# Written-out merge orders for the first three and the last three passes of a software-pipelined transformer kernel

## The chip, the cores and the metric

The kernel runs on one core of a Trainium2 chip. The metric is the device time of one execution in microseconds, as the median of three runs.

## The reference, cut to what matters

There are 32 sequences of 256 tokens with 256 features. For each, a cross attention with 16 heads ("conditioning") is computed from `x` and a second input, and two layers of local attention and gated feed-forward follow; `x` is added at the end.

```
c = cond(x, side, lens)                     # 16 heads, keys masked by length, one own key per query
for l in (0, 1):
    q, k, v = split(shift(c) @ wqkv[l])     # 8 heads of 64
    q, k = rotary_xpos(l2norm(q) * qs, l2norm(k) * ks)
    c = c + local_attention(q, k, v) @ wo[l]       # windows of 128, with a mask
    h = layernorm(shift(c)) * g + b
    a, g = split(h @ w1[l] + b1[l])
    c = c + (a * gelu(g)) @ w2[l] + b2[l]
out = x + c
```

## The kernel before

The work of one sequence is cut into 150 steps in four streams. Stream A (57 steps) is the conditioning: `rows`, `project`, `turn_q`, `part`, `own_key`, 16 `score` and 16 `prob` steps with `split`, `turn_max` and `value` between them, and three `mix` steps. Stream R (24, twelve a layer) projects and rotates q and k: `qk`, `rotate`, `combine`, `turn`. Stream S (48) is the local attention: `value_rows`, `scores`, `normalize`, `turn_probs`, `weigh`, `out_proj`. Stream N (21) is the feed-forward: `mean`, `variance`, six `hidden`, two `down`, and a `finish` that adds `x`.

A step has a part on each engine that takes part in it, and many have none on some engine. The four compute engines each run the steps in an order of their own. `ORDER` (line 124) holds it: four cuts and a string of 150 letters. Each letter takes the next step of its stream. The strings describe one pass. In pass i the kernel does the conditioning of sequence i, layer 0 of sequence i-1 and layer 1 of sequence i-2; steps behind a stream's cut are done one pass later still (`body_of`, line 147). There are 32 sequences and `LAGS` is 3, so 35 passes are written out one behind the other (`run`, line 374). In the first three and the last three of them the same string is used and the steps of sequences that don't exist are left out. So pass 0 holds the conditioning of sequence 0 alone, passes 3 to 31 are full, and passes 32 to 34 hold the layers of the last sequences.

Engines wait for each other by semaphores. Every wait names the sequence and the count that it needs, so another order changes no wait. SyncE has its own fixed order of loads (line 492): in pass i it loads the rows of sequence i+1, and then places the split query and key parts of sequence i in `cQT` and `cKT` by twelve transfers (line 458), each behind the part that it moves: three high key parts, two middle ones, three high query parts, one low key part, two middle query parts, the low query part. The first `score` of a sequence waits for all of them. The low parts are made by GpSimd (`part`, line 549), which also does a power for the norms (`rotate`, line 559), sums in `mean` and `variance` (lines 568, 572) and the parts of the maxima (`split`, lines 537 to 544).

Behind the conditioning of sequence 0 each engine calls its `layers_setup` once (TensorE 88 small matmuls at line 719, the vector engine scalings at lines 1055 to 1094).

Lines that the text speaks of: TensorE `project` 744 to 762, `score` 781, `prob` 799, `value` 809, the mix 820 to 834, `finish` 876, `qk` 894, `value_rows` 908, `turn` 928, `scores` 941, `turn_probs` 950, `weigh` 961, `out_proj` 970, `mean` 980, `variance` 983, `hidden` 994, `down` 1007. Vector engine: `part` 1130, the maxima of `score` 1146, `rotate` 1201 to 1218, `hidden` 1283, `down` 1292. ScalarE: `scores` (exponentials) 657, copy of the turned probabilities 661.

Of the kernel before, what the change touches and what calls it, by code (L numbers as in the profile page):

```python
# [97 lines left out]
def head_steps():  # L98
    steps = []
    for u in range(CH + LAG + 2):  # L100
# [22 lines left out]

ORDER = dict(
    PE=((57, 24, 27, 1),
        "SSARASNASSRRAASRSSAASANRNSSAASNAARARAANAANASANAASANAANSSSSASAASASAAARSRRANARSRNAASRSASARNASASASRRANA"
        "SSASASRASSAARNSNNRNANSSNSASSASASAANSSARSRARRSRANSA"),
    DVE=((56, 22, 27, 1),
        "RAARSSASSSSRRASAANSAASRNSSAANAAAAANASAAANNASANASRRASSAASARSRARASASSNNAARAANSSARRAARRRSNSSAAASAAAAAAA"
        "AAAAAASSSSSRSNNSNNNRNSSSSAAASRNSRNSSRRRSSSSSNRAANS"),  # L130
    Activation=((56, 24, 26, 0),
        "NASARSAANSASSSAAAARSRSAAAAANARAARASSNNRNNANSSANRASNSASASSAASSASASAAAARSASARANRRASRNARSAASAAASRSRSAAS"
        "SSSARSARANANNRRNNNSSSSNNSAASSAASSNASASAASRARSRRRAS"),
    Pool=((52, 11, 43, 0),
        "SSASSSSSSSSSSSSASSRRRAAARRRASARRNNNNNNNARNRRRRRSSAAARAAAAARANRAAARAAASAAARSNRRRNSSSSSASSSSSAAAASRSRA"
        "NNSSSNANNAANNASSSAAAANAASSSSSSASNAAAAAANAAAAASAAAS"),
)


# [4 lines left out]
    N=[(1 + l,) + step for l in range(DEPTH) for step in FEED[l]])  # L144


def body_of(engine):

    cuts, letters = ORDER[engine]
    taken = {}  # L150
    for letter, cut in zip(STREAMS, cuts):
        steps = STREAMS[letter]
        taken[letter] = iter([(lag + 1, name, n) for lag, name, n in steps[cut:]] + steps[:cut])
    body = [next(taken[letter]) for letter in letters]
    assert len(body) == sum(len(steps) for steps in STREAMS.values())
    return body


LAGS = 3


# [27 lines left out]
def adaln_ffn_kernel(nc, x, side, lens, wq, bq, wk, bk, wv, bv, cwo, bo, b_prev, b_self,  # L189
                     wqkv, q_scale, k_scale, wo, ln_g, ln_b, w1, b1, w2, b2, consts, out,  # L190
                     seqs):
    with ExitStack() as ctx:
# [181 lines left out]
        def run(eng, engine, step, layers_setup):  # L374

            body = body_of(engine)

            layers = [False]

            def static(i):  # L380
                for lag, name, n in body:
                    if 0 <= i - lag < seqs:
                        if name not in CONDITIONING and not layers[0]:
                            layers_setup()
                            layers[0] = True
                        step(i - lag, name, n)
                        if (name, n) == CONDITION[-1] and not layers[0]:
                            layers_setup()
                            layers[0] = True

            for i in range(seqs + LAGS):
                static(i)

        def copy_probs(eng, copy, seq, l, h):

# [955 lines left out]
```

## Time and profile before

| | |
|---|---|
| median of three runs | 3763.35 us (3762.83 to 3767.95) |
| profiled execution, its own time | 3767.51 us |
| its span, first to last instruction | 3765.3 us |
| TensorE matmuls busy | 3602.7 us (96%) |
| vector engine busy | 2670.4 us (71%) |
| ScalarE busy | 2242.3 us (60%) |
| GpSimd busy | 788.4 us (21%) |
| mean granted TensorE clock | 0.978 of full |

The names in the profile: PE is TensorE, PEld its weight loads, DVE the vector engine, ACT ScalarE, POOL GpSimd, SP SyncE. Start and duration are in microseconds from the start of the span. A matmul in float32 is recorded as two. Busy time of TensorE counts modelled ends, so it is not a measure of how well a matmul does. Passes in the middle repeat every 111.0 us; the full pass 3 starts near 310 and the last full pass, 31, ends near 3529.

### The profile page before, as it was taken

The numbers are of one execution on the slowest core, as the hardware profiler recorded it, in microseconds if no ns is written. First come the engines' busy times: TensorE is split into PE (matmuls) and PEld (weight loads), VectorE is DVE, ScalarE is ACT, GpSimd is POOL, SyncE is SP. The second block draws the span as 40 slices with busy tenths as digits, with TensorE's granted clock in tenths as the row PEclk, the third lists the DMA queues.
The fourth block names the chain that finished last, engine by engine and source line by source line (L and its number), as shares of the span: only waits on it lengthen the run. The fifth ranks groups of instructions, "written<-read, shape, count | busy, mean of one in ns | idle before, by whom it ended". The sixth has DMA issues, their size and how long they took to land.

```text
span 3765.3 us, 58543 instructions
## 1 busy us (share of the span) xinstructions
PE 3602.7 (96%) x20454; PEld 2447.4 (65%) x20454; DVE 2670.4 (71%) x7188; ACT 2242.3 (60%) x5085; POOL 788.4 (21%) x882
## 2 busy tenths in 40 slices
PE   5789999999999999999999999999999999999987
PEld 2456666666666666666666666666666666666655
DVE  2567777777777777777777777777777777777654
ACT  1246566566566666656656656666665665666653
POOL 1122221222222122222122222212222222222110
PEclk7799999999999999999999999999999999999998
DMA  5111110111111011111101111101111110111000
GB/s 144 23 24 23 29 29 20 16 24 29 29 29 29 14 20 26 29 29 29 23 13 24 30 29 29 29 17 19 24 29 29 29 26 13 21 29 24 7 6 9
DMA packets 104608, 99.34 MB, mean 26 GB/s; under 512 B 15276, under 2 KB 103040, under 8 KB 104320
## 3 DMA queue, kind: packets, MB, share of 16 engines
q1 hardware_dynamic: 104320, 95.61, 13.8%
q8 instruction: 168, 2.75, 0.3%
q14 instruction: 120, 0.98, 0.1%
HBM read 35.80 MB, written 8.39 MB: 12 GB/s over the span
## 4 chain that ended last, share of the span: by engine, by line
PE 85%; DVE 7%; issue 3%; ACT 3%; SPq 1%; POOL 0%; DMA 0%; DVEq 0%; ACTq 0%; POOLq 0%
PE ps L994 15%; PE ps L894 12%; PE ps L1007 9%; PE ps L908 6%; PE ps L941 5%; PE ps L961 5%; PE ps L950 4%; PE ps L809 3%; PE ps L970 3%; PE ps L928 3%; PE ps L752 3%; PE ps L762 3%; PE ps L799 3%; PE ps L781 2%; PE ps L834 2%
## 5 line engine op out<-in xcount | busy, mean ns | idle before, releaser
L559 POOL TENSOR_TENSOR inv<-ssq_f,minus_half 128x16 f32<-128x16 f32 x128 | 419.8, 3279 | 1043.9 <-DVE ssq_f L1209 1040.4
L994 PE MATMUL ps<-feed_area,w_s 128*128 128x256 f32 x2560 | 600.7, 382 | 7.3 <-DVE feed_area L1273 6.3
L994 PEld LDWEIGHTS ps<-feed_area,w_s 128*128 128x128 f32 x2560 | 480.5, 191 | 123.2 <-issue 54.1
L657 ACT ACTIVATE attn_area<-attn_area,f_nb,inv 128x128 f32<-128x128 f32 (+1 forms) x1024 | 546.3, 536 | 13.2 <-DVE f_nb L1237 11.6
L1146 DVE TENSOR_REDUCE c_mx<-ps 128x2 f32<-128x512 f32 x512 | 343.2, 687 | 180.5 <-PE ps L781 179.7
L679 ACT ACTIVATE feed_area<-ps,b_s 128x256 f32<-128x256 f32 x320 | 151.0, 473 | 386.3 <-PE ps L994 384.8
L1007 PE MATMUL ps<-feed_area,w_s 128*128 128x256 f32 x1536 | 355.2, 381 | 5.2 <-DVE feed_area L1283 1.5
L610 ACT ACTIVATE cond_area<-ps 128x512 f32<-128x512 f32 x512 | 294.9, 593 | 104.3 <-PE ps L799 103.4
L1233 DVE CUSTOM_DVE_ANT_0 attn_area<-ps,cst 128x128 f32<-128x128 f32 (+1 forms) x1024 | 303.8, 353 | 72.7 <-issue 71.2
L1007 PEld LDWEIGHTS ps<-feed_area,w_s 128*128 128x128 f32 x1536 | 281.7, 190 | 48.9 <-DVE feed_area L1283 14.6
L1283 DVE SCALAR_TENSOR_TENSOR feed_area<-ps,b_s,feed_area 128x256 f32<-128x256 f32 (+1 forms) x384 | 183.8, 479 | 169.0 <-ACT feed_area L679 166.3
L1248 DVE TENSOR_SCALAR attn_area<-attn_area,f_inv 128x128 f32<-128x128 f32 (+1 forms) x1024 | 284.4, 341 | 9.1
L399 DVE COPY attn_area<-ps 128x384 f32<-128x384 f32 x256 | 142.0, 555 | 200.2 <-PE ps L950 200.2
L648 ACT ACTIVATE attn_area<-ps 128x512 f32<-128x512 f32 x256 | 152.0, 594 | 204.7 <-PE ps L928 201.9
L950 PE MATMUL ps<-cst,attn_area 128*128 128x128 f32 x1536 | 251.1, 280 | 11.8 <-DVE attn_area L1248 11.8
L894 PE MATMUL ps<-wqkv_s,X_ffn 128*128 128x512 f32 x512 | 248.5, 608 | 1.4 <-ACT attn_area L637 1.4
L941 PE MATMUL ps<-attn_area 64*128 64x128 f32 (+1 forms) x2048 | 240.0, 352 | 10.2 <-DVE attn_area L399 5.2
L894 PE MATMUL ps<-wqkv_s,X_cond 128*128 128x512 f32 x512 | 245.8, 602 | 0.1
L961 PE MATMUL ps<-attn_area 128*64 128x256 f32 (+1 forms) x2048 | 227.1, 343 | 18.3 <-ACT attn_area L661 17.9
L970 PE MATMUL ps<-attn_area,wo_s 128*128 128x256 f32 x1024 | 240.6, 384 | 2.6 <-ACT attn_area L665 1.7
L637 ACT ACTIVATE attn_area<-ps 128x512 f32<-128x512 f32 x256 | 151.2, 591 | 152.8 <-PE ps L894 152.7
L549 POOL TENSOR_TENSOR cond_area<-cond_area 128x512 bf16<-128x512 f32 x64 | 102.3, 1598 | 588.8 <-DVE cond_area L1127 395.7
(156 smaller groups left out, 6528.4 us busy)
## 6 DMA issues: line engine op xcount, KB each, us to landing
cond_area<-cond_area SPq DMA_DIRECT2D x384, 128.0 KB, 4.2
x_rows<-in_x SPq DMA_DIRECT2D x32, 256.0 KB, 2.8
f_rows<-in_fside_BxSxS SPq DMA_DIRECT2D x32, 256.0 KB, 3.2
res_rows<-in_x SPq DMA_DIRECT2D x32, 256.0 KB, 2.8
out<-res_rows SPq DMA_DIRECT2D x32, 256.0 KB, 2.1
wqkv_s<-in_L_ffn_wqkv SPq DMA_DIRECT2D x2, 1536.0 KB
w_s<-in_L_ffn_w SPq DMA_DIRECT2D x2, 1364.0 KB
cond_area<-cond_area SPq DMA_DIRECT2D x128, 6.0 KB
```

Source lines behind the costliest of these rows:

```text
L559: nc.gpsimd.tensor_tensor(inv[:, l, t, :], ssq_f[:, l, t, :], minus_half[:, :], ALU.pow).then_inc(SL[l]["inv_norm"], 1)
L610: nc.scalar.activation(cpT[:, u % CPB, :], ps[:, c_bank("prob", u), :], ACT.Exp, scale=float(C_SCALE)).then_inc(S["c_probs"], 1)
L657: nc.scalar.activation(soft[:, h % SOFT, lo:hi], soft[:, h % SOFT, lo:hi], ACT.Exp, bias=f_nb[:, l, q, h:h + 1], scale=inv[:, l, q, h:h + ...
L894: last = mm(ps[:, R0, :], shifted(X_in[l])[:, k, t * P:(t + 1) * P], wqkv_s[:, l, k, c * INNER:(c + 1) * INNER], start=(k == 0), stop=(k = ...
L941: last = mm(ps[:, t_bank("scores", 2 * p + j), q * P:q * P + keys], qT[r:r + FDH, p, q * P:(q + 1) * P], kT[r:r + FDH, p, 0:keys], start=T ...
L950: last = nc.tensor.transpose(ps[:, t_bank(name, h), c * P:(c + 1) * P], soft[:, h % SOFT, c * P:(c + 1) * P], ident)
L961: last = mm(ps[r:r + FDH, t_bank(name, p), lo:N], v_s[:, k, h * FDH:(h + 1) * FDH], pT[:, h % 4, c:c + N - lo], start=(k == 0), stop=(k == 1))
L970: last = mm(ps[:, t_bank(name, m), 0:N], wo_s[:, l, h, m * P:(m + 1) * P], oT[:, h, :], start=(h == 0), stop=(h == HP - 1))
L994: last = mm(ps[:, N0 + f % 2, c * N:(c + 1) * N], w1_s[:, l, k, lo:lo + P], hn[:, k, :], start=(k == 0), stop=(k == KD - 1))
L1007: last = mm(ps[:, N0 + m, 0:N], w2_s[:, l, f, m * P:(m + 1) * P], hid[:, f, :], start=(f == 0), stop=(f == HK - 1))
L1146: V.tensor_reduce(c_mx[:, :, u], ps[:, c_bank("score", u), :].rearrange("p (q k) -> p q k", q=TILES), AX_X, ALU.max).then_inc(S["c_max"], 1)
L1233: V.tensor_tensor_reduce(out=soft[:, h % SOFT, lo:hi], in0=ps[:, t_bank(name, h), lo:hi], in1=mask[:, lo:hi], scale=1.0, scalar=3 * NEG, o ...
```

## The change

The four strings of `ORDER` get new letters. TensorE's, the vector engine's and ScalarE's cuts are the same; GpSimd's cuts change, with two of its working steps exchanged. Two new tables, `HEAD` and `TAIL`, hold for each engine one string for the first three passes together and one for the last three together. `edge_of` builds the list of steps of those passes, stream by stream in the old sequence, and takes them in the order of the letters. The place at which `layers_setup` is called is given by a table (`LAST`): behind the last step of the first conditioning in which the engine works.

```diff
 ORDER = dict(
     PE=((57, 24, 27, 1),
-        "SSARASNASSRRAASRSSAASANRNSSAASNAARARAANAANASANAASANAANSSSSASAASASAAARSRRANARSRNAASRSASARNASASASRRANA"
-        "SSASASRASSAARNSNNRNANSSNSASSASASAANSSARSRARRSRANSA"),
+        "SSARASNSSASASARSARSAANARRNNSAANNAANAASAARASSSRANAAASASSSANSAASSAARSARAANARRASRNAASRASSARNARRNASSAASA"
+        "ARSSSAASSRASAANNSNNNSSNSSAASSARSAASSARSRNRARSRANSA"),
...
-    Pool=((52, 11, 43, 0),
...
+    Pool=((57, 10, 22, 0),
...
+HEAD = dict(
+    PE=(
+        "AAAAAAAAAAAAAAAAAAAAAAAAAAAAAAAAAAAAAAAAAAAAAAAAAAAAAAAAAARARRAAARRSARARASAARRRRAARAAAAASAASAAAAAAAA"
...
+TAIL = dict(
+    PE=(
+        "SSRSSSSRSRSSRSRSNSSSSSSSRSSRNSNRSRRSNRNRNSNSNSNNRSSNSRSSSRRRNSNRSNNNNSNSRSSNSSSSSNSSRSRRNRSRSNSSSSSS"
+        "NSSSSSNSNNNNSSNNSSSSSSSNRNRSRRRNNRRSRNRNRRNRSNSNSSSSSSSSSNSSSSSSSSSNSSNNNNNNNNNNN"),
...
+def edge_of(engine, passes, letters, seqs):
+
+    lists = passes_of(engine)[0]
+    taken = {letter: [(i - lag, name, n) for i in passes for lag, name, n in steps if 0 <= i - lag < seqs]
+             for letter, steps in lists.items()}
+    assert sorted(letters) == sorted(letter for letter, steps in taken.items() for step in steps)
+    taken = {letter: iter(steps) for letter, steps in taken.items()}
+    return [next(taken[letter]) for letter in letters]
+
+LAST = dict(PE=(0, "mix", 2), DVE=(0, "mix", 1), Activation=(0, "mix", 2), Pool=(0, "split", GROUPS - 1))
...
-            for i in range(seqs + LAGS):
-                static(i)
+            steps = edge_of(engine, range(LAGS), HEAD[engine], seqs)
+            for i in range(LAGS, seqs):
+                steps += [(i - lag, name, n) for lag, name, n in body]
+            steps += edge_of(engine, range(seqs, seqs + LAGS), TAIL[engine], seqs)
+            for seq, name, n in steps:
+                step(seq, name, n)
+                if (seq, name, n) == LAST[engine]:
+                    layers_setup()
```

What the letters say, in the steps in which an engine works. Of TensorE's 127 in a full pass the largest move is by 9 places, the mean by 1.2. `weigh` 0 of layer 1 comes right behind `scores` 2 (before, `qk` and two `project` stood between). On ScalarE the copy of turned probabilities 1 of layer 1 now stands ahead of `variance` of layer 0, and `qk` 0 behind the `part` of the key.

Head, behind the first conditioning: TensorE does `qk` 0.0, `project` 0, `qk` 0.1, `project` 1, 2, `qk` 1.0, `value_rows` 0, `turn_q`, `qk` 1.1, `project` 3, `value_rows` 1, `project` 4, three `turn`, `score` 0 and 1, the fourth `turn`; before, `turn` and `value_rows` came behind `score` 11. The vector engine does `rotate` 0 ahead of `project` 1 and `rotate` 1 ahead of `project` 3; before, `rotate` 1 came behind `score` 9. GpSimd does its part of `rotate` 0 ahead of the key's `part`, and that of `rotate` 1 ahead of `own_key`. At the end of pass 1 `mix` 0 stands ahead of the output projection, and `mean` behind `mix` 2. Pass 2 is alike for sequence 1.

Tail: sequence 29's layer-1 attention comes ahead of most of sequence 30's layer-0 feed-forward, whose last four `hidden` and `down` stand between the `turn` and `scores` steps of sequence 31. In pass 33 the vector engine does `rotate` 1 of sequence 31's layer 1 behind `hidden` 1 of sequence 30, where it stood behind `hidden` 5 and both `down`; TensorE does the first `qk` ahead of `variance`, and `hidden` 5, `down` 0, `down` 1 and `finish` of sequence 30 between the attention steps of sequence 31.

## Rows read from the trace of the kernel before

**Rows 1.** Page, the span and part 1: busy us, share, instructions.
```profile
span 3765.3 us, 58543 instructions
PE 3602.7 (96%) x20454; PEld 2447.4 (65%) x20454; DVE 2670.4 (71%) x7188; ACT 2242.3 (60%) x5085; POOL 788.4 (21%) x882
```

**Rows 2.** Windows: stretch, length, busy us of each engine, clock, DMA share, GB/s.
```profile
22.80:101.70 78.90, 46.36 (x203) 21.46 (x203) 23.95 (x58) 16.02 (x30) 6.77 (x19) 0.61 0.41 90
...
122.50:213.00 90.50, 66.53 (x347) 38.08 (x347) 46.73 (x121) 34.21 (x84) 16.46 (x23) 0.81 0.16 24
213.00:310.00 97.00, 87.58 (x473) 54.79 (x473) 64.66 (x155) 48.90 (x107) 23.00 (x25) 0.95 0.16 23
...
1975.00:2086.00 111.00, 110.04 (x638) 75.26 (x640) 82.98 (x223) 70.06 (x159) 24.40 (x27) 1.00 0.14 25
...
3529.00:3623.40 94.40, 85.47 (x429) 57.42 (x428) 59.62 (x173) 56.47 (x129) 15.29 (x7) 1.00 0.02 7
3623.40:3665.90 42.50, 33.39 (x175) 25.18 (x175) 19.48 (x77) 21.37 (x53) 1.45 (x2) 0.88 0.00 0
3665.90:3704.90 39.00, 31.47 (x118) 20.47 (x118) 18.56 (x26) 13.69 (x22) 7.28 (x3) 0.96 0.02 8
3704.90:3736.60 31.70, 21.47 (x104) 14.25 (x105) 13.08 (x66) 13.49 (x42) 0.72 (x1) 0.68 0.03 9
3736.60:3765.30 28.70, 19.01 (x76) 14.90 (x76) 7.69 (x12) 6.52 (x10) 0.72 (x1) 0.86 0.03 10
```

**Rows 3.** Waits of TensorE, 1975 to 2086: us in total, times, longest.
```profile
PE ps L961 <- ACT attn_area L661: 0.3, 1, 0.3
```

**Rows 4.** Order of time, TensorE and vector engine, passes 0 and 1: start, us, instruction.
```profile
59.03 2.69 DVE L1146 TENSOR_REDUCE c_mx<-ps 128x2 f32<-128x512 f32 x4 [17.92 <-PE ps L781]
...
73.31 0.69 DVE L1146 TENSOR_REDUCE c_mx<-ps 128x2 f32<-128x512 f32 x1 [0.70 <-PE ps L781]
...
135.67 0.69 DVE L1130 TENSOR_TENSOR cond_area<-ps,cond_area 128x512 f32<-128x512 f32 x1 [1.38 <-ACT cond_area L598]
...
145.93 1.03 PE L781 MATMUL ps<-cond_area 97*128 97x256 bf16 x4 [5.76 <-DMA cond_area<-cond_area]
...
157.94 1.22 DVE L1201 TENSOR_TENSOR attn_area<-attn_area,cos_t 128x1024 f32<-128x1024 f32 x1
...
161.74 1.23 DVE L1218 TENSOR_TENSOR attn_area<-attn_area 128x1024 f32<-128x1024 f32 x1
...
173.54 0.69 DVE L1146 TENSOR_REDUCE c_mx<-ps 128x2 f32<-128x512 f32 x1 [2.17 <-PE ps L781]
```

**Rows 5.** Lines 549, 559, 1209 by themselves: shortest, median, longest ns.
```profile
L549 POOL TENSOR_TENSOR cond_area<-cond_area x64: 1152/1158/2073, 32.6 to 3435.8; 128x512 bf16<-128x512 f32 x64
...
L559 POOL TENSOR_TENSOR inv<-ssq_f,minus_half x128: 3270/3278/3291, 140.3 to 3698.8; 128x16 f32<-128x16 f32 x128
...
L1209 DVE TENSOR_SCALAR ssq_f<-ssq x128: 174/175/1111, 139.1 to 3698.6; 128x16 f32<-128x16 f32 x128
```

**Rows 6.** Order of time, TensorE and vector engine, layer 1 of sequence 31.
```profile
3669.90 2.83 PE L894 MATMUL ps<-wqkv_s,X_ffn 128*128 128x512 f32 x4
...
3676.07 1.22 DVE L1201 TENSOR_TENSOR attn_area<-attn_area,cos_t 128x1024 f32<-128x1024 f32 x1 [2.94 <-ACT attn_area L637]
...
3690.29 5.45 PE L1007 MATMUL ps<-feed_area,w_s 128*128 128x256 f32 x24 [0.35 <-DVE feed_area L1283]
...
3696.18 1.22 DVE L1201 TENSOR_TENSOR attn_area<-attn_area,cos_t 128x1024 f32<-128x1024 f32 x1
...
3704.88 0.93 PE L941 MATMUL ps<-attn_area 64*128 64x128 f32 x8 [0.73 <-issue]
...
3729.80 5.39 PE L970 MATMUL ps<-attn_area,wo_s 128*128 128x256 f32 x16 [0.57 <-ACT attn_area L665]
```

**Rows 7.** Order of time, one full pass, around the turned probabilities of layer 1.
```profile
1981.66 0.93 PE L941 MATMUL ps<-attn_area 64*128 64x128 f32 x8
...
1983.91 0.48 ACT L661 ACTIVATE attn_area<-ps 128x384 f32<-128x384 f32 x1
```

More of the change, by code:

```diff
@@ new lines @@
+        "RSSRARSSANANNRNNRNSNSSSSNAAASSSSNAASAARASARSSRRRAS"),
+    Pool=((57, 10, 22, 0),
+        "RRSSSSRRRRSSRSSRRRRNNNAARRNARANNNSSSSRANSASSSAASASSRRRRNNAAAAAAASSSSASAASSSASSSSSSSSSSSSSSSSSSSSSARR"
+        "AAAAANNNRRNNAAAAAAARNNAAANNANANAAAAAAAAAAAAAAAAAAA"),
+)
+HEAD = dict(
+    PE=(
+        "AAAAAAAAAAAAAAAAAAAAAAAAAAAAAAAAAAAAAAAAAAAAAAAAAAAAAAAAAARARRAAARRSARARASAARRRRAARAAAAASAASAAAAAAAA"
+        "ASAAAAAAAAAAASSAAASAAAASSSSAAASAAAASSASSSSSSASSASANARAANAARSAARRRNRARRSANARARANARAANAANARAANSAAANASA"
+        "NASSSASAASAARASSSAASAAASASASSRAARRASARSSASAASRAASRASAAARASRARRASRNASA"),
+    DVE=(
+        "AARARAAAAAAAAAAAAAAAAASAAAAAAAAAAAAAAAAAAAAAAAAAAAAAASAAAAAAAAAARAAARARRRARRARAAAAAAAARARSAAAAAAAAAA"
+        "AARAAAAASAASARASAAAAASASAAAAAASSASSSSSSSSASASAASSSASNAAAAAANRARRRRNASAAAARNNASARARRRARNAANAANAAASNAS"
+        "SRSSNAAASAASSAAAASAAASSSASASAAAAASAASASAAAASRSRRAAASSSRRRRARSAASNS"),
+    Activation=(
+        "AAAAAAAAAAAAAAAAAAAAAAAAAAAAAAAAAAAAAAAAAAAAAAAAAAAAAAAAAARAARRRRAAAARRARRRRAAAAAARAASAASSAAAAAAAAAA"
+        "AAAAAAAAAAAASASAASSAASAASSAASASAAASSSSSAASSSSASANASRAANRAAAAARSRRSRRNRRAAAAAAASANNANRRANRNANAAAASAAS"
+        "ASSNSAAAAASASASAASASRAASASSSSARARASAASSSRRASAAARSAAASARARSRAARARSR"),
+    Pool=(
+        "RRASSAASAASASSASSSSSSSAAAASAAAAAAAAAAAAAAAAAAAAAAAAAAAAASAASAAAAARAAAAAARRRSSAAASSSSAAASSSSSSSSSASSS"
+        "SSASSASSSSSSSSAARRRRRAAAAAAAAAAAAAAAAAARAAAARAAAAAAAAAAAAANNANANNRNNNNANAAAAAAAAAAAAAAAAAARRRRAAAAAR"
+        "RAAAAAARRAAAAAAAAAAAAAAAAAAAAAAAAAAAAAAAAAAAAAAAA"),
+)
@@ L144, with passes_of, body_of @@
     N=[(1 + l,) + step for l in range(DEPTH) for step in FEED[l]])
-def body_of(engine):
+def passes_of(engine):
     cuts, letters = ORDER[engine]
-    taken = {}
+    lists = {}
     for letter, cut in zip(STREAMS, cuts):
         steps = STREAMS[letter]
-        taken[letter] = iter([(lag + 1, name, n) for lag, name, n in steps[cut:]] + steps[:cut])
+        lists[letter] = [(lag + 1, name, n) for lag, name, n in steps[cut:]] + steps[:cut]
+    return lists, letters
+def body_of(engine):
+    lists, letters = passes_of(engine)
+    taken = {letter: iter(steps) for letter, steps in lists.items()}
     body = [next(taken[letter]) for letter in letters]
```

30 lines of the change are left out of this document (13 added, 17 removed).

## The prediction

> **What bounds the kernel now.** I began with the page's busy lines. TensorE is busy 3602.7 of 3765.3 us, 96% [rows 1]. So at most 4% can be won, and what matters is where the rest lies. The second view is the windows by pass, with the granted clock of each [rows 2]. A pass in the middle takes 111.00 us with TensorE busy for 110.04, 0.96 less, and the longest wait in it is 0.3 us [rows 3]. The edges are looser. Pass 0 takes 78.9 us for 46.4 of busy time, pass 1 90.5 for 66.5, pass 2 97.0 for 87.6; behind the last full pass stand 94.4, 42.5, 39.0, 31.7 and 28.7 us, with 85.5, 33.4, 31.5, 21.5 and 19.0 busy. That leaves 7.5 to 32 us of idle TensorE in a stretch, and some of the work is done at the half clock. The third view is the order of time around two places, one at each end [rows 4, 6], since what ends the wait there is the head of another engine's queue.
>
> **The change part by part.** No instruction, wait or transfer is added or removed; every engine runs the same steps in another order. Costs are therefore waits that appear or go.
>
> Pass 0 (to 101.7) and the layer setup: the first 50 working steps of TensorE are in the old order, and those of the other engines too. The new place of the setup call is behind the same work. Nothing hides this, as nothing moves: 0 us.
>
> Pass 1, forecast -10 us. Before, the first score of sequence 1 waits for the placing transfers until 145.93, with TensorE idle 5.76 us; later the vector engine leaves the maxima to rotate tile 1 from 157.94 to 163.0, and TensorE stands [rows 4]. New: all four projections of q and k, the values, and both rotations come ahead of the first score. What this costs: rotation 0 now stands ahead of two bias additions and of the query's part on DVE, and GpSimd's power (3.28 us, rows 5) ahead of the key's last part, on which SyncE's placing queue waits in order. The query's rest ended at 136.4; with a rotation of 5 us, which I let begin at 131, the two bias additions, the turn and the copy, I put it at 139.5. The last placing is then issued some 2.5 us later, the first score at 148 to 149, the first maximum 3.5 us later than before (rotation 1 and the own key lie ahead of it). What it gives: the maxima then run with no rotation and no q/k turns among them, at the pace of pass 0, where the first of fourteen starts at 59.03 and the last at 73.31; 3.5 us late from the old 146.5 (the end of the first score's two matmuls), with one tile of masking (1.5) among them, the fourteenth ends near 167 and not past 174. That is -7. Behind it, an output projection now lies between the two turns of the mix, where TensorE waits for the vector engine, and the mean no longer stands ahead of the last projection; I put the two at -3, out of the idle time of rows 2. Ends: +3.5 (only the delay comes true) and -24 (all of the idle time goes, rows 2).
>
> Pass 2, -2 us. The same front-loading, but beside a feed-forward, so only 9.4 us are idle at all (97.0 less 87.6, rows 2). Ends +2 and -9.4; I stay near the low end because the maxima and both rotations still share DVE.
>
> At this place a clash between two engines bears on the sum. GpSimd's subtraction takes between 1.15 and 2.07 us, and the vector engine's clamp, 0.17 us in most places, up to 1.11 [rows 5]; the long ones stand beside work of the other engine. The new head puts a rotation beside the query's last part again, and both long forms are already in the 2.5 us of delay. By the Trainium skill, SBUF — State Buffer, "Who interferes with whom", the two share a port pair under an exclusive lock and the second to issue is blocked for the whole of the first. By that rule each further clash adds up to 1 us and pass 1 would give 8 or 9 and not 10; the rows agree with it so far as the 1.11 against 0.17 goes.
>
> Full passes (29 of them), -3 us, that is -0.1 a pass. TensorE moves its steps by 1.2 places on average and 9 at most. The floor is 110.04 busy, so the new order can give at most the 0.96, and I bound it by 0.7 a pass, -20 in all. The places that could cost: the second weighing (weigh 0 of layer 1) now follows straight on the third pair of scores, where before a projection and two more lay between; hidden tiles 1 and 2 come back to back; the first score comes about 0.8 us earlier. For the first, ScalarE's copy of the turned probabilities started at 1983.91, while the scores behind the turn started at 1981.66 and take 0.9 [rows 7]: in the old ScalarE order weighing would stall 1.9 us. But ScalarE's order moves with it: the copy now comes ahead of the square root and its table load, and q's copy behind it, so it starts near 1982.0 and ends at 1982.5, just in time. The other two have a cover: a whole hidden tile between one's matmuls and the use of its bank, and no wait on a transfer in rows 3. I take a small gain; ends -20 and +12 (0.4 us a pass, a little more than the one wait of rows 3).
>
> Tail to the end of the last layer-0 feed-forward (3529 to 3665.9), -3.5 us. Order changes, total does not: TensorE's work is the same up to the last output projection of that layer. Attention of sequence 29 runs first and with less beside it, which loses some us; sequence 31's scores come 6 us earlier and find their waits filled. The mean moves three steps up and the variance comes ahead of a normalization on the vector engine; 1.5 us for that is an estimate out of the 9.1 idle. Idle now: 8.9 and 9.1 us (rows 2), so -18 is the far end, +4 the other.
>
> Last layer, -12.5 us, the surest term. Before, DVE rotates tile 0 of sequence 31 at 3676.07 and tile 1 only at 3696.18, behind six hidden products and two down additions of sequence 30, and TensorE does the scores at 3704.88 [rows 6]. New: the first projection follows the mean at 3666.4 (before, 3669.90, behind the variance), which moves rotation 0 to 3672.5. Rotation 1 stands behind only two hidden products. Its input needs four projections, one block of values and two hidden tiles: 24 matmuls of the down projection take 5.45 us, so such a piece of eight (or four twice as wide) 1.8, seven of them 12.7, and with copy and square it starts near 3681 and ends at 3686. TensorE's own work sets about the same date: 31.5 us are busy in the old stretch (rows 2), the two down additions' matmuls (5.45) and the finish leave it, so with no wait it would be through 25 us after 3665.9. I put the scores at 3690, and that is -14.5. The down projection and the finish, 6 us of work, fall into the attention that follows, where TensorE is idle 10.2 of 31.7 us: I charge +2 for them. The output projection then starts near 3717 where it started at 3729.80, and what follows (mean to store, 28.7 us) is unchanged. Ends -16 and -5.
>
> Here the clock is a row of its own: 0.68 of full from 3704.9 to 3736.6, and 0.86 behind it, where the passes in the middle have 1.00 [rows 2]; TensorE is idle a third of that stretch. I take no gain from it, since I used it up in charging only 2 us for 6. The Trainium skill, TensorE: Matmul & The Clock Gate, "What's actually happening", says that the gate sets the rate by how busy the array has lately been; by it the fuller stretch would run more at 2.4 GHz, and the term would be -16.
>
> Sum: 0 - 10 - 2 - 3 - 3.5 - 12.5 = -31 us on the profiled execution of 3767.5 us (span 3765.3 and 2.2 around it), so 3736.5. The median of the three runs is 3763.35, 4.2 below that one; the same step gives 3732 us.
>
> **The rivals.** (1) *The full pass pays too.* For it: TensorE is idle 0.96 us in each of 29 passes. Against: the pass is within 1% of its busy time. -20 in place of -3: 3715. (2) *Only the tail pays.* In the head the rotation ahead of the placing costs what it saves, since the serial chain of one sequence's conditioning took 78.9 us alone in pass 0. Only the tail's -16 remains: 3748. Against it: pass 1 waits for a rotation in the middle of its maxima. (3) *The orders do not do what they say*: the letters that move are mostly steps for which an engine only waits anyway, and the chain of sequence 31 keeps its length; about -3, 3760. Against: the gap between the two rotations is 20 us in one row pair. (4) *The full pass stalls, and the kernel is slower.* The place is the second weighing behind ScalarE's copy; the price 1.9 us, the whole distance in the old rows, 29 times: 55 - 28 = +27, 3790. It decides from 0.97 us a pass (28/29). Against it: ScalarE's new order puts the copy first.
>
> **How the numbers follow.** Forecast 0.55; (1) 0.14; (2) 0.16; (3) 0.07; (4) 0.08. A difference under 0.2%, 7.5 us, can't be told from none. Faster: 0.55 + 0.14 + 0.16 = 0.85; same 0.07; slower 0.08. The likeliest case alone would lie within 3722 to 3743. The range must take in part of (1) and most of (2): 3712 to 3751, which leaves out (3), (4) and a little of (1).
>
> **What would show it.** Right: pass 1 ends near 203 and not 213; the distance of two like steps in the middle stays between 110.7 and 111.1; the two rotations of the last layer stand within 10 us of each other; from the last output projection to the end still 35.5 us. Wrong: a wait of weighing on ScalarE's copy in every pass, or a first score later than 150. A full pass over 111.5 us would overturn the forecast.

## The result and the profile after

The changed kernel takes 3718.26 us (median of four runs, 3715.13 to 3719.79), the one before 3765.51 us beside it (3762.83 to 3767.95). The ratio is 0.9871 with a 95% interval of 0.9860 to 0.9883: 1.3% faster. I had predicted 3732, so the kernel gained 47 us where I had 31. An execution can fall into a slower state (one of the five of kernel 12 below took 3994.8 us at a mean clock of 0.885, and is left out); the times compared here are without it.

The page of the changed kernel has the same instructions in a shorter span, but for one load of ScalarE's function tables (252 loads of 1.28 us where there were 253). TensorE's busy time fell by 14.8 us for the same matmuls; its mean granted clock went from 0.978 to 0.983:

```profile
span 3716.3 us, 58542 instructions
PE 3587.9 (97%) x20454; PEld 2439.0 (66%) x20454; DVE 2668.0 (72%) x7188; ACT 2230.2 (60%) x5084; POOL 766.6 (21%) x882
```

The windows of the changed kernel, cut at the same steps as [rows 2]. The columns are stretch, length, then busy us (and instructions) of TensorE, its weight loads, the vector engine, ScalarE and GpSimd, the granted clock, the share of busy DMA engines and GB/s:

```profile
22.80:101.30 78.50, 47.24 (x216) 23.77 (x216) 24.03 (x58) 16.54 (x32) 6.80 (x19) 0.63 0.41 91
122.04:197.71 75.67, 66.01 (x347) 36.36 (x347) 47.56 (x121) 33.97 (x83) 14.03 (x22) 0.83 0.20 29
197.71:282.15 84.44, 81.93 (x472) 53.28 (x473) 65.90 (x158) 48.90 (x108) 23.43 (x26) 1.00 0.16 26
1946.20:2057.10 110.90, 110.00 (x638) 75.11 (x636) 82.83 (x223) 69.69 (x160) 23.73 (x27) 1.00 0.15 25
3499.10:3592.60 93.50, 85.25 (x431) 57.64 (x430) 60.89 (x173) 55.96 (x130) 16.76 (x9) 1.00 0.02 7
3592.60:3634.50 41.90, 33.20 (x174) 25.13 (x174) 19.03 (x76) 20.77 (x52) 0.72 (x1) 0.88 0.00 0
3634.50:3657.90 23.40, 22.09 (x84) 14.34 (x84) 16.39 (x22) 13.12 (x20) 7.28 (x3) 1.00 0.00 1
3657.90:3681.70 23.80, 17.79 (x120) 12.23 (x121) 13.35 (x68) 14.24 (x43) 0.00 (x0) 1.00 0.00 1
3681.70:3716.30 34.60, 23.51 (x93) 18.31 (x92) 9.23 (x15) 6.51 (x10) 1.45 (x2) 0.84 0.07 23
```

Set against [rows 2], with the places of [rows 6] for the last layer, three stretches hold nearly all of it:

| stretch | before | after | difference | forecast |
|---|---|---|---|---|
| start to end of setup | 122.5 | 122.0 | -0.5 | 0 |
| pass 1 | 90.5 | 75.7 | -14.8 | -10 |
| pass 2 | 97.0 | 84.4 | -12.6 | -2 |
| 29 full passes | 111.00 each | 110.93 each | -2.1 | -3 |
| tail, up to the last layer's mean | 136.9 | 135.4 | -1.4 | -3.5 |
| last layer, mean to output projection | 63.9 | 47.2 | -16.8 | -12.5 |
| output projection to the end | 35.5 | 34.6 | -0.9 | 0 |
| sum | | | -49.0 | -31 |

The sum is the difference of the two spans, 3765.3 and 3716.3 (the rows are rounded); the medians differ by 47.3.

In order of time, the two chains that I had followed in [rows 4] and [rows 6] (start, us, engine and line; in brackets the idle time before and what ended it), first in pass 1:

```profile
131.85 1.23 DVE L1247 TENSOR_TENSOR attn_area<-attn_area,cos_t 128x1024 f32<-128x1024 f32 x1
...
141.19 1.76 DVE L1247 TENSOR_TENSOR attn_area<-attn_area,cos_t 128x1024 f32<-128x1024 f32 x1 [0.56 <-ACT attn_area L683]
...
149.83 0.61 PE L827 MATMUL ps<-cond_area 97*128 97x256 bf16 x4 [1.02 <-DMA cond_area<-cond_area]
...
167.19 0.69 DVE L1192 TENSOR_REDUCE c_mx<-ps 128x2 f32<-128x512 f32 x1 [0.70 <-PE ps L827]
```

Both rotations now come ahead of the first score, which starts at 149.83 (it was 145.93), and the fourteenth maximum at 167.19 (it was 173.54). The second rotation's first product takes 1.76 us and not 1.23, as GpSimd's part of the query runs beside it (from 140.70, for 1.16): the clash of [rows 5], with the longer form now on the vector engine. Then in the last layer:

```profile
3641.79 1.22 DVE L1247 TENSOR_TENSOR attn_area<-attn_area,cos_t 128x1024 f32<-128x1024 f32 x1
...
3649.22 1.23 DVE L1247 TENSOR_TENSOR attn_area<-attn_area,cos_t 128x1024 f32<-128x1024 f32 x1 [0.69 <-ACT attn_area L683]
...
3657.94 0.93 PE L987 MATMUL ps<-attn_area 64*128 64x128 f32 x8 [0.73 <-issue]
...
3662.01 2.86 PE L1053 MATMUL ps<-feed_area,w_s 128*128 128x256 f32 x12
...
3672.66 2.86 PE L1053 MATMUL ps<-feed_area,w_s 128*128 128x256 f32 x12
...
3681.71 0.67 PE L1016 MATMUL ps<-attn_area,wo_s 128*128 128x256 f32 x2
```

The rotations are 7.4 us apart where they were 20.1, and the two down projections of sequence 30 (L1053) stand between sequence 31's scores and weighings. The windows show the same as counts: TensorE does 84 matmuls from the mean to the scores where it did 118, and 120 from the scores to the output projection where it did 88. The second stretch got no longer by that.

### The profile page after: what moved, and what is told of

The parts are those of the page before. It is cut to its first block, busy times and chain, and to the rows that moved or that the text cites. A ratio compares the mean times of both kernels' runs of the same rounds, so it can differ in the third digit from the quotient of the medians.

```text
span 3716.3 us, 58542 instructions
## 1 busy us (share of the span) xinstructions
PE 3587.9 (97%) x20454; PEld 2439.0 (66%) x20454; DVE 2668.0 (72%) x7188; ACT 2230.2 (60%) x5084; POOL 766.6 (21%) x882
## 3 DMA queue, kind: packets, MB, share of 16 engines
q1 hardware_dynamic: 104320, 95.61, 14.5%
## 4 chain that ended last, share of the span: by engine, by line
PE 91%; DVE 3%; ACT 2%; issue 1%; SPq 1%; POOL 1%; DMA 0%; ACTq 0%; DVEq 0%; POOLq 0%
PE ps L1040 15%; PE ps L940 12%; PE ps L1053 9%; PE ps L1016 6%; PE ps L954 6%; PE ps L1007 5%; PE ps L987 5%; PE ps L996 4%; PE ps L845 3%; PE ps L855 3%; PE ps L974 3%; PE ps L798 3%; PE ps L827 3%; PE ps L808 3%; PE ps L880 2%; PE ps L790 2%
## 5 line engine op out<-in xcount | busy, mean ns | idle before, releaser
L1192 DVE TENSOR_REDUCE c_mx<-ps 128x2 f32<-128x512 f32 x512 | 349.2, 689 | 167.2 <-PE ps L827 163.6
L1053 PE MATMUL ps<-feed_area,w_s 128*128 128x256 f32 x1536 | 355.8, 381 | 10.8 <-DVE feed_area L1329 10.8
L1053 PEld LDWEIGHTS ps<-feed_area,w_s 128*128 128x128 f32 x1536 | 281.6, 190 | 59.0 <-DVE feed_area L1329 23.4
L694 ACT ACTIVATE attn_area<-ps 128x512 f32<-128x512 f32 x256 | 152.2, 594 | 259.6 <-PE ps L974 253.8
L1294 DVE TENSOR_SCALAR attn_area<-attn_area,f_inv 128x128 f32<-128x128 f32 (+1 forms) x1024 | 258.4, 315 | 9.1
L987 PE MATMUL ps<-attn_area 64*128 64x128 f32 (+1 forms) x2048 | 239.2, 351 | 11.6 <-DVE attn_area L445 7.5
L996 PE MATMUL ps<-cst,attn_area 128*128 128x128 f32 x1536 | 229.9, 276 | 6.5 <-DVE attn_area L1294 6.5
L1016 PEld LDWEIGHTS ps<-attn_area,wo_s 128*128 128x128 f32 x1024 | 189.1, 190 | 44.2 <-issue 21.1
L1007 PEld LDWEIGHTS ps<-attn_area 128*64 128x64 f32 x2048 | 125.3, 136 | 138.9 <-issue 87.4
```

The source lines that it names most:

```text
L987: last = mm(ps[:, t_bank("scores", 2 * p + j), q * P:q * P + keys], qT[r:r + FDH, p, q * P:(q + 1) * P], kT[r:r + FDH, p, 0:keys], start=T ...
L996: last = nc.tensor.transpose(ps[:, t_bank(name, h), c * P:(c + 1) * P], soft[:, h % SOFT, c * P:(c + 1) * P], ident)
L1007: last = mm(ps[r:r + FDH, t_bank(name, p), lo:N], v_s[:, k, h * FDH:(h + 1) * FDH], pT[:, h % 4, c:c + N - lo], start=(k == 0), stop=(k == 1))
L1016: last = mm(ps[:, t_bank(name, m), 0:N], wo_s[:, l, h, m * P:(m + 1) * P], oT[:, h, :], start=(h == 0), stop=(h == HP - 1))
L1053: last = mm(ps[:, N0 + m, 0:N], w2_s[:, l, f, m * P:(m + 1) * P], hid[:, f, :], start=(f == 0), stop=(f == HK - 1))
L1192: V.tensor_reduce(c_mx[:, :, u], ps[:, c_bank("score", u), :].rearrange("p (q k) -> p q k", q=TILES), AX_X, ALU.max).then_inc(S["c_max"], 1)
```

## The experiments

Most kernels below are the changed one with the step list of each engine put together from two orders, `new` (the change's) and `OLD` (the table of the kernel before). Unless said otherwise a kernel was run once, with a profile, and is read by its stages. The stages repeat well: pass 1 in the new order takes 75.0 to 75.7 us behind an unchanged pass 0 (76.9 once), pass 2 84.4 or 84.5. Two stages do not. Pass 0 with the setup, whose steps are the same in kernels 1 to 9, ends between 118.6 and 125.4 us, and its end goes with the clock from 80 to 105 us: granted 0.77 in kernels 5 and 1 (ends 118.6 and 119.1), 0.70 in the changed kernel (122.0), 0.50 in kernels 6 and 7 (124.6 and 125.4). And the tail, from the last `rows` to the end, takes 324.6 to 328.8 us in its new order. So the whole time of a single run is uncertain by some 3 us either way, and a comparison of two whole times by more; the stage is what counts.

**1 to 4: one stage at a time back in its old order.**

```
 def plan(engine, seqs):
-    return new_head(engine) + full(engine, ORDER) + new_tail(engine)
+    return new_head(engine) + full(engine, ORDER) + old(engine, (32, 33, 34))         # 1
+    return new_head(engine) + full(engine, OLD) + new_tail(engine)                    # 2
+    return old(engine, (0, 1)) + new_head(engine)[CUT:] + full(...) + new_tail(...)   # 3
+    return new_head(engine)[:CUT] + old(engine, (2,)) + full(...) + new_tail(...)     # 4
```

> The changed kernel with the last three passes in the pass order of the kernel before; head and full pass stay new. Theory (the stages' gains are independent and add): the last three passes take back what the two traces show for them, 1.4 us before the last layer's mean, 16.8 in the last layer and 0.9 behind the output projection, so the profiled execution is some 19 us over that of the changed kernel (3718.5), 3737.6, with the rotations of the last layer some 20 us apart on VectorE again. Rival (the last layer gains only because what is ahead of it has a new pace): under 10 us, below 3729.

> The changed kernel with passes 3 to 31 in the pass order of the kernel before; head and tail stay new. Theory: the distance of like steps goes from 110.93 back to 111.0 us, 2 us in 29 passes, 3720.5. Rival (a forecast's case: the full pass pays by itself through the scores' and copies' waits): over 111.2 us a pass, 3727 or more. Head and last layer keep their times to 0.5 us.

> The changed kernel with the first two passes in the pass order of the kernel before, pass 2 in the new head's order. Theory (each pass of the head gains for itself): pass 1 takes 90.5 us again instead of 75.7, pass 2 stays near 84.4, so 3733.4. Rival (pass 2 is shorter because pass 1 has left its engines nearer to each other, or its work has come earlier): pass 2 lengthens as well, by up to 12.6 us, 3746.

> The changed kernel with pass 2 alone in the pass order of the kernel before. Theory (pass 2 was not near its floor of work; its own order is what gains): it takes 97 us again instead of 84.4, with TensorE idle for some 15 us in it and its clock below full speed in part, so 3731. Rival (the gain of pass 2 was inherited from pass 1): pass 2 stays under 88 us, at most 3722.

| kernel | time | over the changed kernel's profiled 3718.6 | expected | its stage |
|---|---|---|---|---|
| tail old | 3737.28 | +18.7 | +19 | last `rows` to the end 327.1 -> 349.3 (kernel before: 346.2) |
| full passes old | 3721.68 | +3.1 | +2 | 110.97 -> 111.03 a pass |
| passes 0, 1 old | 3733.18 | +14.6 | +14.8 | pass 1 75.7 -> 91.1, pass 2 84.4 |
| pass 2 old | 3729.45 | +10.9 | +12.6 | pass 2 84.4 -> 97.2, pass 1 76.9 |

The four whole times add up to 47.4 us, where the medians differ by 47.3. That this comes so close is luck: read by their own stages the four give 22.2 + 1.7 + 15.4 + 12.8 = 52.1 us, where the spans differ by 49.0. In kernel 1 pass 0 ended 2.9 us earlier than in the changed kernel, and its old tail took 3.1 us more than the same order in the kernel before; in kernel 4 the new tail took 2.5 us less. Within that, each stage gains for itself: pass 2 keeps its 84.4 us behind an old pass 1, and takes 97.2 behind a new one. The rivals by which pass 2 or the last layer inherits its gain are out. (The distance per pass is taken here over 28 passes from pass 3 to the last `rows`; 0.06 us a pass are 1.7 us in all, so most of kernel 2's +3.1 is its tail, 1.7 us longer.)

**5 and 9: how much of pass 2's new order is needed.** I took the rotation ahead of the scores for the reason, then the early start of the attention.

```
     was, new = old(engine, (2,)), new_head(engine)[CUT:]
-    return head + new
+    steps = new[:new.index(LAST_NEW[engine]) + 1]     # 5: last turn / combine of sequence 1
+                                                      # 9: first weigh (PE, ScalarE), third scores (DVE)
+    return head + steps + [s for s in was if s not in steps]
```

> The changed kernel, with pass 2 in the new order only up to the step in which sequence 1's queries and keys have been rotated and turned; the rest of the pass follows in the order of the kernel before. Theory (pass 2 was held up by sequence 1's attention coming late, so the early rotation is the larger part): most of the 12.8 us by which pass 2 differs between 97.2 (pass 2 in its old order) and 84.4 is back, the pass takes 86 to 89 us, in all 3719 to 3722. Rival (what gains is how the scores, weighings and the second layer's first steps are spread over the conditioning's last 8 heads): the pass stays over 93 us, 3727 or more.

> As the kernel whose pass 2 was new up to sequence 1's rotated keys (its pass 2 took 97.4 us, as with the old order), but new up to the first weighing of sequence 1's attention; the rest of the pass in the order of the kernel before. Theory (what pass 2 gains is that sequence 1's attention starts between heads 8 and 11 of sequence 2's conditioning instead of behind head 13, and so fills waits of TensorE there): half or more of the 12.8 us is back, pass 2 takes 86 to 91 us, in all 3719 to 3724. Rival (it is the spread of the later weighings and of the second layer's first steps): the pass stays over 94 us.

Both theories fell. Pass 2 takes 97.4 us with the new front and 97.0 with the new order up to the first weighing, against 97.2 with none of it. The whole times are 3728.67 and 3732.86. The windows of kernel 9 from 40 us into the pass, in slices of 10 us (columns as above):

```profile
238.40:248.40 10.00, 8.84 (x63) 5.66 (x60) 7.90 (x33) 7.45 (x25) 0.81 (x4) 1.00 0.01 4
248.40:258.40 10.00, 6.79 (x39) 2.88 (x38) 2.96 (x8) 5.95 (x15) 0.55 (x3) 0.99 0.00 1
258.40:268.40 10.00, 9.72 (x58) 5.27 (x59) 9.02 (x26) 3.21 (x8) 3.84 (x3) 0.84 0.01 2
268.40:278.40 10.00, 6.31 (x40) 3.65 (x41) 4.77 (x11) 7.05 (x19) 0.00 (x0) 0.68 0.00 0
```

The same slices of the changed kernel, whose pass begins 0.7 us earlier:

```profile
237.70:247.70 10.00, 9.81 (x65) 6.51 (x64) 8.21 (x37) 7.45 (x24) 0.23 (x2) 1.00 0.01 2
247.70:257.70 10.00, 9.70 (x77) 5.53 (x76) 7.39 (x28) 9.02 (x26) 1.39 (x7) 1.00 0.00 1
257.70:267.70 10.00, 10.00 (x64) 6.37 (x63) 6.72 (x10) 6.31 (x13) 3.59 (x2) 1.00 0.01 2
267.70:277.70 10.00, 9.53 (x73) 5.44 (x71) 8.73 (x13) 5.83 (x12) 3.97 (x2) 1.00 0.01 2
```

Up to 50 us into the pass the two do the same (63 and 65 matmuls in the slice, 241 and 243 since the pass began). Kernel 4, with all of the pass old, had done 213 by then, so the new first part does put work ahead. Then kernel 9 does 39 where the changed kernel does 77 (and kernel 4 does 59), which uses up most of the lead, and 40 against 73 at the end, with the clock down at 0.68. In order of time, vector engine, ScalarE and TensorE of kernel 9:

```profile
255.54 0.69 DVE L1260 TENSOR_REDUCE c_mx<-ps 128x2 f32<-128x512 f32 x1 [6.39 <-PE ps L895]
...
269.51 0.48 ACT L771 ACTIVATE attn_area<-attn_area,f_nb,inv 128x128 f32<-128x128 f32 x1
...
271.89 0.47 ACT L775 ACTIVATE attn_area<-ps 128x384 f32<-128x384 f32 x1
...
272.51 1.54 PE L1075 MATMUL ps<-attn_area 128*64 128x256 f32 x8 [3.69 <-ACT attn_area L775]
```

The first row is the cost of the old order's next steps: TensorE puts two second-layer projections (1.98 us each) and a value product ahead of `score` 14, the vector engine idles 6.39 us for it, and everything that it owes sequence 1 comes later. That wait belongs to the seam between the two orders: the longest of its kind is 2.3 us in kernel 4. The others are where it is paid: ScalarE's copy of turned probabilities (L775) stands behind the exponentials of the fourth head pair (L771, four of them, from 269.51), those start only then because their scores came late, and TensorE stands 3.69 us for the copy. The kernel with all of pass 2 old has this wait too, 3.3 us at the same place. In the changed kernel these exponentials start at 252.12 and no wait of the pass is over 1.3 us. So the gain needs the new order behind the first 50 us of the pass, where the last two head pairs of sequence 1 and the second layer's first projections lie. Whether that part would gain without the new first part no kernel tests, and which single step decides is open.

**6: the part ahead of the power, on GpSimd.** Tests my reason for the later first score of pass 1.

```
 for seq in (1, 2):                       # GpSimd, head
-    ... (seq - 1, "rotate", (0, 0)), (seq, "part", 1), ...
+    ... (seq, "part", 1), (seq - 1, "rotate", (0, 0)), ...
```

> The changed kernel; in the head, GpSimd splits the normed rows of sequences 1 and 2 (part) ahead of the power of the rotation of the sequence before, not behind it. Theory (GpSimd's queue held up the placing, so the scores of sequence 1 began at 149.8 and not at 147): the first score of pass 1 comes 1 to 3 us earlier and pass 1 shortens by as much, 3715.5 to 3717.5. Rival (the placing waits for its own descriptors and VectorE's half, not for GpSimd): no change at the first score, 3718 to 3719.

3719.67 us. GpSimd's part of the key starts 9.2 us after the pass begins where it started 15.7 after, and ends 5.5 us earlier. The first score comes 27.1 us after the pass begins (151.76 less 124.62), against 27.8 (149.83 less 122.04), and the pass takes 75.0 us and not 75.7. Both lie within what the unchanged head shows (26.7 to 27.9 and 75.0 to 76.9 us in kernels 1, 2, 4, 5, 7, 8 and 9). So no gain is to be seen, the rival is right for the stage, and GpSimd's queue is not what holds the first score (what does is not shown); the whole misses both cases only because pass 0 ended at 124.6. The part now falls beside the rotation on the vector engine and takes 2.24 us:

```profile
133.77 2.24 POOL L664 TENSOR_TENSOR cond_area<-cond_area 128x512 bf16<-128x512 f32 x1 [54.55 <-DVE cond_area L1242]
```

Elsewhere it takes 1.16 us. That is the clash of [rows 5], and it eats 1.1 of the 6.6 us by which the step starts earlier.

**7: the last rotation moved on the vector engine alone.** My forecast called that rotation the surest term.

```
 tail = old(engine, (32, 33, 34))         # as kernel 1
+if engine == "DVE":                      # sequence 31, layer 1
+    move combine tile 0, rotate tile 1 ahead of hidden 2 of sequence 30
```

> The kernel with the last three passes in their old order (3737.3), with one move on VectorE: the combine of sequence 31's first rotated tile and the rotation of its second, both of layer 1, stand ahead of the third gate of sequence 30. Theory (as the forecast had it, VectorE's late rotation holds up the last layer): the two rotations come within 10 us of each other and the scores come some 12 us earlier, 3725. Rival (the order of TensorE and ScalarE holds it just as long, since their turns still stand behind the feed-forward of sequence 30): at most 3 us, 3734 or more.

3748.29 us, 11.0 over kernel 1: neither. Of these 11.0 the last layer, from its mean to the end, makes up 8.0 (109.1 against 101.0, and 99.4 in the kernel before); the rest is a pass 0 that ended 6.3 us later, less 3.5 us between the last `rows` and the mean, both in steps that the two kernels share. Its vector engine, in order of time:

```profile
3643.71 0.69 DVE L1388 TENSOR_TENSOR feed_area<-feed_area 128x512 f32<-128x512 f32 x1
3649.92 1.23 DVE L1316 TENSOR_TENSOR attn_area<-attn_area,cos_t 128x1024 f32<-128x1024 f32 x1 [5.52 <-ACT attn_area L752]
...
3660.81 1.23 DVE L1316 TENSOR_TENSOR attn_area<-attn_area,cos_t 128x1024 f32<-128x1024 f32 x1 [2.15 <-ACT attn_area L752]
...
3665.77 0.87 DVE L1398 SCALAR_TENSOR_TENSOR feed_area<-ps,b_s,feed_area 128x256 f32<-128x256 f32 x2
```

The moved rotation waits for ScalarE's copy of the projection (L752), which TensorE's and ScalarE's old orders make late, and the gates of sequence 30 (L1398) wait behind it; TensorE then stands 4.9 us for one of them. The rotations come 10.9 us apart instead of 20, and the last layer is slower. The scores start 47.3 us after the mean (3684.48 less 3637.14), 6.8 later than in kernel 1. So the rotation moved alone loses, and the gain needs the other engines' orders with it; the early projections are the likeliest of these, but they were not moved by themselves.

**8: the old tail with a fuller TensorE.** Prices the clock in the old last layer.

```
 # kernel 1, TensorE, sequence 31, layer 1
+if name in ("scores", "turn_probs", "weigh"):
+    6 x matmul(bank nobody reads, identity, identity)   # 128 columns, bf16
```

> The kernel with the last three passes in their old order (3737.3), and 6 unused bf16 matmuls of 128 columns ahead of each scores, turn and weighing step of TensorE for sequence 31 in layer 1, into a bank that nobody reads. Theory (part of the old last layer's loss is the clock, granted at 0.66 there): the granted clock from scores to output projection goes to 0.9 or more and the stretch of 25 us shortens by 1 to 3 us, 3734 to 3736. Rival (TensorE's clock plays no part there, the stretch is a chain over VectorE and ScalarE): the added matmuls cost what they take, 3738 to 3741.

The windows from scores to output projection, of kernel 1 and then of this one:

```profile
3674.70:3699.70 25.00, 16.18 (x89) 10.16 (x89) 12.23 (x64) 13.55 (x42) 0.00 (x0) 0.66 0.04 11
```

```profile
3675.00:3700.00 25.00, 19.24 (x187) 14.40 (x186) 12.23 (x64) 14.21 (x43) 0.00 (x0) 0.86 0.04 12
```

The clock rises from 0.66 to 0.86, short of the 0.9 that I had asked for, and the distance from the first score to the output projection goes from 24.9 to 24.0 us: 1.0, the low end of the theory. The whole, 3737.61, does not show it, since this run's pass 0 ended at 123.0 and the other's at 119.1.

In the changed kernel the down projections of sequence 30 do the same with useful work, and there chance has made a cleaner comparison. Ten of the kernels here have the new last layer. In seven of them this stretch was granted 1.00 throughout and takes 23.8 us; in kernels 2, 5 and 9, with the same steps, it was granted 0.93 and takes 25.3 to 25.4. Kernel 5:

```profile
3667.23:3692.61 25.38, 19.42 (x121) 13.26 (x121) 13.41 (x67) 14.32 (x43) 0.00 (x0) 0.93 0.00 1
```

So 1.6 us hang on whether the clock drops in that stretch, and the same order doesn't always keep it up.

**10 to 12: pass 0, which the change left alone.** It ends, with the setup, at 122 us; TensorE is idle 18.2 us for the placing's transfers, and behind the conditioning come 15.3 us of small sums that nothing runs beside.

```
 # 10, SyncE
-load_layer(0); load_layer(1); load_scales(); ... place_parts(0)
+load_layer(0); ... place_parts(0); load_layer(1); load_scales()
 # 11, as 10, TensorE: 2 of the 22 sums behind each of score 12..15 and prob 5..11 of sequence 0,
 #     vector engine: the weights' scaling behind its score 9, the bias part behind split 3
 # 12, as 11, TensorE: matmuls of 128 columns into an empty bank
+fill(70) ahead of score 0; fill(6) ahead of score 1..11; fill(60) ahead of prob 0; fill(5) ahead of each sum
+fill(8), fill(12), fill(16) ahead of the last mean, variance, hidden 0
```

> The changed kernel; SyncE issues the weight loads of the second layer and the two rows of scales behind the first placing of sequence 0, not ahead of it. Theory (TensorE's wait of 18.2 us before its first score, at 58.0, is for the placing's transfers, which stand behind all the weights): the first score comes 10 us or more earlier, and pass 0 ends 6 to 12 us earlier, 3707 to 3713. Rival (the second layer's weights then come late for the layers' setup behind pass 0, or the transfers share the same bandwidth): under 3 us, 3716 or more.

> The kernel with the early placing, and the layers' setup (the weights' sums on TensorE, 88 small matmuls and 15.3 us behind pass 0, and VectorE's part of it) in pieces between the scores and weighings of sequence 0. Theory (in pass 0 the engines wait for one another, so the setup fits in there, and behind it it stands by itself): 15 to 20 us less than with the early placing alone, 3690 to 3698. Rival (the setup's pieces stand on the chain of pass 0): 0 to 5 us less, 3703 or more.

> The kernel with the early placing and the spread setup (3706.2), and unused bf16 matmuls of 128 columns into a bank that stands empty in pass 0: 70 ahead of its first score, 6 ahead of scores 1 to 11, 60 ahead of the first weighing, 5 ahead of each of the 22 sums; and 8, 12 and 16 ahead of the last layer's last mean, variance and first hidden step. Theory (in that kernel TensorE has a granted clock of 0.50 from 46 to 112 us, also where it is busy 98% of the time with sums of one column, so it lacks columns and not work): the clock there goes to 0.8 or more, the sums take half as long and pass 0 ends 6 to 12 us earlier, and the last feed-forward saves about 1 us, 3693 to 3700. Rival (the other engines set the pace of pass 0, or the clock stays low): the unused matmuls cost what they take, 3706 to 3715. Timed in five rounds against the kernel before, which stands at 3763 to 3766: ratio 0.981 to 0.983 by the theory.

Kernel 10 ran in 3712.5 us, 11 in 3706.2. Pass 0 with the setup ends at 116.2 and 111.8, both ahead of the 118.6 to 125.4 of the kernels with the old pass 0. In kernel 10 the first score comes at 46.41 (it was 58.01), so the theory is right, at the low end of its range; a later wait takes back some 7 of the 11.6 us won:

```profile
46.41 1.03 PE L898 MATMUL ps<-cond_area 97*128 97x256 bf16 x4 [7.62 <-DMA cond_area<-cond_area]
...
60.54 0.59 PE L916 MATMUL ps<-cond_area 100*128 100x256 bf16 x2 [6.95 <-DMA cond_area<-cond_area]
```

The rows of maxima that the first weighing needs are now queued behind the second layer's weights. Kernel 11 keeps that wait and hides part of the sums; it gains 4.4 us in pass 0 over kernel 10, where I had 15 to 20, so the rival is right (0 to 5 us, 3703 or more). The clock is 0.50 from 46 to 112 us in it. Kernel 12 was to mend that and didn't, and came out beyond both of my cases: four executions take 3703.5 to 3723.1 us, a ratio of 0.9868 (0.9847 to 0.9889) to the kernel before, no better than the change's 0.9871, and in the profiled one pass 0 ends at 123.9. Its windows:

```profile
46.00:60.00 14.00, 11.14 (x128) 9.85 (x128) 6.38 (x11) 0.37 (x1) 1.62 (x8) 0.80 0.82 273
60.00:80.00 20.00, 17.92 (x121) 13.91 (x122) 6.23 (x25) 4.71 (x9) 0.81 (x4) 0.54 0.02 4
80.00:95.00 15.00, 15.00 (x101) 14.15 (x99) 1.50 (x4) 2.11 (x4) 0.82 (x4) 0.50 0.00 1
95.00:104.00 9.00, 9.00 (x65) 7.46 (x63) 0.00 (x0) 2.23 (x5) 0.00 (x0) 0.50 0.00 1
```

Up to 60 us the clock did rise (0.80, where kernel 11 had 0.50). From there it is 0.50 although TensorE has no idle time at all from 80 to 104, so the added matmuls cost more than I had counted: five of them take 0.69 us there, where six take 0.50 at full clock in kernel 8. The last feed-forward saved 0.3 us (33.7 against 34.0 in kernel 11). Kernel 11 is thus the best candidate, 12 us under the changed kernel by one run. Pass 0 gives 10.2 of these against the changed kernel's profile, and 6.8 against the earliest end of an old pass 0; more than that the single run does not show.

## Why the prediction was right, and where not

The direction, the places and the range held; the size was 16 us short. Pass 1, pass 2 and the last layer gave more than I had forecast, pass 2 by far the most.

*Pass 0, 0 us.* Right, -0.5; the same steps vary by more than that from run to run (118.6 to 125.4).

*Pass 1, -10 us; it was -14.8.* The steps up to the fourteenth maximum came as worked out: first score 149.8 (I had 148 to 149), the maximum at 167.2 (167). Within the pass the score is 4.4 us later and the maximum 5.9 earlier. For the later score I had named two causes, and kernel 6 rules out GpSimd's power; the rotation ahead of the bias additions is left, untested. The part behind the maximum is off, where I put -3 and -8.9 came: from the fourteenth maximum to the end the old pass takes 39.5 us with 29.6 busy, the new 30.5 with 26.2. So 3.4 of the 8.9 us is TensorE work that now stands ahead of the maximum (204 matmuls are left where there were 222), and 5.5 are waits that went. The order of time of the kernel before shows waits there that I had not looked at, here the weighing's on ScalarE's copy and the scores' on the vector engine:

```profile
175.83 0.93 PE L941 MATMUL ps<-attn_area 64*128 64x128 f32 x8 [0.84 <-DVE f_mx L1233]
...
179.24 0.39 PE L781 MATMUL ps<-cond_area 97*128 97x256 bf16 x2 [1.16 <-ACT cond_area L610]
...
194.62 0.87 PE L961 MATMUL ps<-attn_area 128*64 128x256 f32 x8 [1.80 <-ACT attn_area L661]
```

In the changed kernel the longest wait behind the fourteenth maximum is 1.0 us. I had priced only the mix and the mean. That these waits went because of the moved steps is read from the two traces; no kernel puts back the rear of pass 1 alone.

*Pass 2, -2 us; it was -12.6.* This is the term that failed, beyond even its far end of -9.4. I wrote that I stay near the low end "because the maxima and both rotations still share DVE". Kernel 4 gives 12.8 us for this pass alone. Two things were wrong. The far end was the idle time of [rows 2], and TensorE's busy time is no floor where the clock is not full: it went from 87.6 to 81.9 us for the same matmuls as the clock went from 0.95 to 1.00. That is 5.7 us beside 6.9 of idle time. (An estimate gives the clock 3.7 of the 5.7: in the old pass the slice from 253 to 263 us was granted 0.83 with 8.7 us busy, that from 283 to 293 was granted 0.66 with 6.6, and the others nearly all 1.00. The rest is open.) And I looked at the front of the pass, where kernels 5 and 9 show that the new order gives nothing by itself; what it needs behind that, the order of the second half, I never costed.

*Full passes, -3 us; it was -2.1,* and the full passes of kernel 2 give 1.7. The distance of 110.9 is inside the 110.7 to 111.1 that I asked for. The weighing did not stall behind ScalarE's copy; the longest waits of TensorE in the pass from 1946.2 are (us in total, times, longest):

```profile
PE ps L1053 <- DVE feed_area L1329: 0.3, 1, 0.3
PE ps L987 <- DVE attn_area L445: 0.2, 1, 0.2
```

*Tail to the last mean, -3.5 us; it was -1.4.* The right side, under half the size, and no more than the same steps vary by: from the last `rows` to the last mean the new order takes 243.6 to 246.1 us, the old one 244.8 to 248.3.

*Last layer, -12.5 us; it was -16.8.* Mean to scores gave -15.6 for my -14.5. From the scores to the output projection I charged +2 for the down projections and took nothing for the clock; it was -1.1, at a clock of 1.00 where it was 0.66. Kernel 8 puts a clock of 0.86 there at 1.0 us, and the changed order itself takes 1.6 us more where it is granted 0.93 (kernels 2, 5 and 9), so a third to a half of my 3 us of error is the clock, and the profiled execution was one of those that got it in full; the rest is that the inserted work fell wholly into waits (17.8 busy of 23.8 us). The sentence that gave -16 by the Trainium skill, TensorE: Matmul & The Clock Gate, "What's actually happening", came nearer than my sum, and the clock did go to 2.4 GHz in the fuller stretch. The mechanism I named was incomplete: kernel 7 shows that the rotation moved by itself makes the last layer 8 us longer.

*What follows the output projection,* "unchanged": -0.9, and 33.7 to 34.6 us in all ten kernels with the new tail, where the kernel before and kernels 1 and 8 take 35.5.

*The signs.* The weighing's stall did not come, the two rotations stand 7.4 us apart, and the first score came at 149.8, 0.2 us from the 150 that I had called a sign of being wrong. Pass 1 ended at 197.7, well ahead of the 203 that I had. "No instruction is added or removed" was off by the one table load.

*The rivals.* "Only the tail pays" is out by kernels 3 and 4, "the orders do not do what they say" and the stall by the result. "The full pass pays too" gave about the right time (3715), for a wrong reason: the full passes gave 2 us, and what went beyond the forecast came from pass 2, the last layer and pass 1.

## What to carry to other kernels

Price a stretch of idle time and low clock by what its matmuls take at full clock (instructions times the duration of the same line in the steady part), and not by its busy time: the floor lies lower than the trace's busy sum says. In a kernel with an order written out for every engine, a step moved on one engine alone can cost more than it was to bring (8 us in the last layer here), and the first part of a new order can bring nothing without the rest (97.0 and 97.4 us against 97.2); move the whole chain. Test by putting one stage back at a time, and read the stage and not the whole time: steps that nobody touched moved whole times by up to 6.8 us here. Read the waits of the whole pass, not only the first of them.

## What the runs showed of the hardware

TensorE stayed at 1.2 GHz (granted 0.50) from 80 to 104 us in kernel 12 with no idle time, and in the changed kernel's setup behind pass 0 the same is seen. The first row is the changed kernel, the other two are the setup of the kernel before:

```profile
104.00:111.80 7.80, 7.80 (x39) 7.80 (x39) 0.00 (x0) 0.00 (x0) 0.00 (x0) 0.50 0.00 0
...
102.00:104.50 2.50, 2.50 (x25) 2.50 (x24) 0.00 (x0) 0.58 (x2) 0.00 (x0) 1.00 0.00 0
105.50:115.00 9.50, 9.50 (x47) 9.50 (x46) 0.00 (x0) 0.00 (x0) 0.00 (x0) 0.50 0.00 0
```

The setup consists of matmuls of one column, each behind a load of 128x128 weights. In the kernel before they began at full clock, ten of them in a microsecond, and the clock fell to 0.50 among them, with no idle time before or behind it. In kernel 12 a third of the 166 matmuls of the stretch are such (59); 73 are the added bf16 matmuls of 128 columns, and those did not lift the clock. The Trainium skill, TensorE: Matmul & The Clock Gate, "What's actually happening", has the rate set by how busy the array has been; by the profile's busy share this stretch disagrees, and the measurement stands. In kernel 11 the float32 matmuls of 128 to 512 columns behind pass 0 began at 0.50 (111.8 to 115.0), and the clock was 0.94 from 115 to 120 and 1.00 from there. What it is in those matmuls that keeps the clock low is open.
